# Prologue of a convolution and attention kernel: halves of the taps and of the first image's inputs on other engines, scales inside the first convolution

## The chip, the cores and the metric

One core of one Trainium2 chip. The metric is device time in microseconds of one execution; the median over runs is compared. TensorE multiplies matrices, VectorE (DVE), ScalarE (ACT) and GpSimd (POOL) work element by element, and SyncE (SP) issues DMAs. Each engine takes its instructions in the order in which they are written, and semaphores order the engines among each other.

## The reference

The input `x` is 16 images of 256 channels of 64 x 64 float32. Two layers, each with a residual:

```
x = x + L0(gn(x))    # rotated 3x3 convolution in 8 groups of 32 channels
x = x + L1(gn(x))    # linear attention with cubed features, 8 heads, and a 5x5 depthwise convolution of v
L0: pooled = mean(x); angles = tanh(mlp(pooled)) * pi/4
    w = bilinear rotation of base_kernel by the image's angle
    out = grouped_conv(x, w) * sigmoid(mlp2(pooled))
L1: q, k = relu(x Wq + bq), relu(x Wk + bk), both over softplus(scale_param), cubed, with the norm kept
    out = (q (k^T v) z + depthwise5x5(v)) Wproj + bproj
gn: normalisation over 32 groups of channels
```

## The kernel before

Channels lie on partitions. Factors of matrix products are held as two float16 parts, a high half (rounded) and a low half (what is left), and a product is three matmuls (high x high, high x low, low x high); each operand is scaled by a power that comes from its maximum (`a_w` for the projection's weights, `a_t` for the taps, `a_p`, `a_r`, `a_o`).

The work is written out by hand, engine by engine. A loop over images runs the attention of image b together with the convolution of image b+2. Ahead of it stands the prologue, which is all that the change touches; it handles images 0 and 1 in full and the statistics of image 2. Its parts, in order:

1. Statistics of image 0 (`pixel_stats`, `deviations`, `spreads`, `variance`, `tail`), its pooled means and two small MLPs (`squash` on ScalarE is their tanh, sigmoid and sines), the rotation of its kernel on GpSimd (`rotation(0)`, 27 steps in a chain), and the blocks of rotated weights written to BD by DMA (`weights` on SP's queue, `late_weights` on ScalarE's, 8 issues each; `wt_in` counts them).
2. `softplus` of the head scales, on VectorE with two `exponentials` on ScalarE.
3. The same statistics and MLPs for image 1.
4. `largest_taps`, `largest_weights`, `largest(1)`, `largest_biases`, `scales`: chains of VectorE instructions in which each waits for the one before it. `largest(1)` is two round trips to TensorE.
5. The first convolution (image 0): 8 groups g of two halves q. `high(c, g)` on VectorE zeroes the borders of a plane and casts it to float16, `conv_low` on GpSimd makes its low half, `convolve` is 12 matmuls of 512 columns into bank VA[q], `conv_out` evicts it into the pixels, `result_stats` takes statistics, `shift` on ScalarE adds a bias, `store_x1` stores. Planes have three slots: `high(0, g+3)` waits until both halves of group g are convolved. `rotation(1)` runs on GpSimd meanwhile, with `conv_low(0, 3..7)` between its steps.
6. The second convolution (image 1), the statistics of image 2, and from group 4 on the attention inputs of image 0: units of 512 positions in two slots, each normalised on ScalarE (`attn_input`), cast to its high half on VectorE, its low half on GpSimd, after which SP may load the unit two further on (`next_unit`).
7. `squash(2)` and the first `squares` of the loop.

The taps of the depthwise convolution (`toeplitz`, 12 chunks of 128 x 1024 float32) come through three slots (PL and two parts of SL). ScalarE makes the high half of a chunk (`taps`), VectorE the low half (`low_taps`), and SP loads the chunk three further on when the low half is there (`load_taps`). Scaled weights are split likewise (`split`, `split_bias`): ScalarE the high halves, VectorE the low ones.

Of the kernel before, what the change touches and what calls it, by code (L numbers as in the profile page):

```python
# [5 lines left out]
def conv_then_focused_attention(  # L6
# [58 lines left out]
    with ctx:  # L65
# [129 lines left out]
        t_rdy, tp_act, tp_rdy = sem("t_rdy"), sem("tp_act"), sem("tp_rdy")  # L195
# [59 lines left out]
        TPM = TP[:, :, :, :, :].rearrange("p c k a n -> p (c k) a n")  # L255
        KS = K23[:, :, :, :].rearrange("p k a n -> p k (a n)")
# [64 lines left out]
        def _(sp):  # L321
# [22 lines left out]
            def load_taps(i):  # L344
                if i >= 3:
                    sp.wait_ge(tp_rdy, i - 2)
                    carry(sp)
                sp.dma_start(taps_tile(i), toeplitz[:, i * PIX:(i + 1) * PIX]).then_inc(taps_in[i % 3], 16)
# [60 lines left out]
            def first_convolution():  # L409
                for g in range(3):  # L410
                    planes_after(0, g + 3, g + 1)
                for g in range(GROUPS):
                    if 1 <= g <= 5:
                        for i in (2 * g + 1, 2 * g + 2)[:CHUNKS - 2 * g - 1]:
                            load_taps(i)
# [12 lines left out]
            def second_convolution():  # L428
# [6 lines left out]
                for s in range(4):  # L435
                    sp.wait_ge(x1_out[s], X1_IN * 2)
                    carry(sp)
                for u in range(2):
                    load_unit(0, u)
# [14 lines left out]
                sp.wait_ge(tp_rdy, CHUNKS)  # L454
                carry(sp)
# [75 lines left out]
            for g in range(4):  # L531
                sp.wait_ge(s0_rdy, 2 * g + 2)
                carry(sp)
                load_stats(1, g)
            sp.dma_start(dt32, dw_taps[0, :].partition_broadcast(P)).then_inc(t_in, 16)
            sp.dma_start(DWB[:, :], dw_b[0, :].partition_broadcast(P)).then_inc(t_in, 16)
# [5 lines left out]
            for g in range(4, GROUPS):  # L542
                sp.wait_ge(s0_rdy, 2 * (GROUPS + g - 4) + 2)
                carry(sp)
                load_stats(1, g)
            for i in range(3):
                load_taps(i)
# [4 lines left out]
            for g in (0, 1):  # L552
                load_stats(2, g)
            weights(0)
# [158 lines left out]
        def _(dve):  # L713
# [81 lines left out]
            def largest_taps():  # L795
# [6 lines left out]
                over(a_t, m_t, 16384.0)  # L802
                dve.sem_inc(t_rdy, 1)
# [30 lines left out]

            def low_taps(i):
                dve.wait_ge(tp_act, i + 1)
                hi, lo = (TPM[:, 8 * i:8 * i + 8, a, :] for a in range(2))
                v.scalar_tensor_tensor(lo, taps_tile(i).rearrange("p (m n) -> p m n", m=8), a_t, hi,
                                       ALU.mult, ALU.subtract).then_inc(tp_rdy, 1)
# [118 lines left out]
            def high(c, g):  # L958
# [8 lines left out]
                if g >= slots:  # L967
                    dve.wait_ge(conv_full, 2 * (GROUPS * c + g - slots) + 2)
                dve.wait_ge(cx_rdy, 6 * (GROUPS * c + g + 1))
# [16 lines left out]

            def attn_input(c, u, h):
                dve.wait_ge(xn_rdy, c * 2 * NU + HALVES * u + h + 1)
                hi = XHL[:, 0, h, u * UNIT:(u + 1) * UNIT].rearrange("p (y m x) -> p y m x", y=4, m=4)
                v.tensor_copy(hi, U[:, u % 2, h].rearrange("p m y x -> p y m x")).then_inc(h_rdy, 1)  # L990
# [181 lines left out]
            modulation_back(0)  # L1172
            for g in range(3):
# [9 lines left out]
            largest_taps()  # L1183
            dve.wait_ge(w_in, 16 * N_W)
            largest_weights()
            largest(1)
            largest_biases()
            scales()

            for g in range(GROUPS):  # L1190
                for q in range(2):
# [6 lines left out]
                    if q == 1 and g < 2:  # L1198
                        split(g, wq32[:, g, :], WQ[:, 0, g, :], WQ[:, 1, g, :], a_w)
                    if q == 1 and g == 2:  # L1200
                        split(2, wp32, WP[:, 0], WP[:, 1], a_p)
                    if q == 1 and g == 3:
# [608 lines left out]
```

## Time and profile before

| what | value |
|---|---|
| median of 3 runs | 3855.68 us (3854.17 to 3865.21) |
| profiled execution, its own time | 3868.91 us |
| its span, first to last instruction | 3867.1 us |
| TensorE, busy share of the span | 91% |
| VectorE | 71% |
| ScalarE | 69% |
| GpSimd | 41% |
| mean granted TensorE clock | 0.978 |

The busy times are means over the whole kernel, of which the prologue is the first 265 us; the loop over images has the rest. A row of the timeline is one instruction or several of one form in a row; what stands in brackets is how long the engine was idle before it, and what ended that.

### The profile page before, as it was taken

How to read it: one execution, taken by the hardware profiler on the slowest of the kernel's cores; microseconds unless marked ns; L12 is line 12 of the kernel's file. 1: busy time of each engine (PE TensorE's matmuls, PEld its weight loads, DVE VectorE, ACT ScalarE, POOL GpSimd, SP SyncE). 2: the span in 40 equal slices, each digit the busy share in tenths (PEclk: the TensorE clock that was granted, in tenths of full speed). 3: DMA queues.
4: the chain of work that ended last, by engine and by line, in shares of the span. 5: the costliest groups of instructions: out<-in, count | busy, mean ns of one | idle time of the engine just before them, and what ended most of it. 6: DMA issues, size and time to landing. Idle time of an engine off the chain costs nothing.

```text
span 3867.1 us, 94623 instructions
## 1 busy us (share of the span) xinstructions
PE 3532.3 (91%) x27988; PEld 2857.3 (74%) x27988; DVE 2762.7 (71%) x6715; ACT 2651.2 (69%) x7096; POOL 1596.4 (41%) x1557
## 2 busy tenths in 40 slices
PE   1679999999999999999999999999999999999897
PEld 1248787777877778787777878777787777878786
DVE  7776776767677676777767677676767767575747
ACT  2347676766777677677766767676676767677675
POOL 4551443615345261544526254361535436150402
PEclk9889999999999999999999999999999999999999
DMA  6652634436353453635446263443626344360302
GB/s 217 210 182 73 187 118 139 141 116 177 101 171 111 138 170 91 192 112 151 128 122 190 78 189 112 141 144 114 194 79 184 111 137 135 92 184 13 110 12 77
DMA packets 560058, 516.59 MB, mean 134 GB/s; under 512 B 97601, under 2 KB 491969, under 8 KB 559553
## 3 DMA queue, kind: packets, MB, share of 16 engines
q1 hardware_dynamic: 555200, 508.99, 43.6%
q8 instruction: 230, 3.77, 0.4%
q14 instruction: 276, 2.25, 0.2%
q10 hardware_dynamic: 4352, 1.57, 0.2%
HBM read 351.06 MB, written 134.22 MB: 125 GB/s over the span
## 4 chain that ended last, share of the span: by engine, by line
PE 57%; DVE 12%; issue 11%; ACT 9%; DMA 6%; POOL 2%; SPq 2%; DVEq 1%; ACTq 0%; POOLq 0%
PE F L1541 11%; PE SM L1524 9%; PE VAB L1541 7%; PE F L1580 6%; PE T L1552 5%; PE VAB L1580 5%; DMA PL<-xp 5%; PE PP L1632 4%; PE VAB L1610 3%; ACT K L1308 3%; PE F L1543 2%; PE T L1601 2%; DVE F L996 1%; PE T L1620 1%; SPq L352 1%
## 5 line engine op out<-in xcount | busy, mean ns | idle before, releaser
L1541 PE MATMUL F<-WQ,XHL 128*128 128x256 f16 x6144 | 817.3, 274 | 27.4 <-ACT V L1345 19.1
L636 POOL TENSOR_TENSOR SL<-PL,SL 128x1122 f16<-128x1122 f32 x112 | 259.8, 2320 | 1067.2 <-DVE SL L970 1067.2
L661 POOL TENSOR_TENSOR XR<-XR,V 128x512 f32<-128x512 f32 x256 | 325.9, 1273 | 898.0 <-DVE XR L1057 898.0
L1541 PEld LDWEIGHTS F<-WQ,XHL 128*128 128x128 f16 (+1 forms) x6144 | 601.0, 98 | 103.7 <-issue 33.7
L1314 ACT ACTIVATE K<-K,SCAL 128x256 f32<-128x256 f32 x1024 | 512.6, 505 | 192.2 <-DVE K L1002 191.8
L1308 ACT ACTIVATE K<-F,SCAL 128x256 f32<-128x256 f32 x1024 | 474.8, 469 | 242.9 <-DVE F L996 240.0
L1524 PE MATMUL SM<-SL,BD 128*128 128x512 f16 x2688 | 634.9, 385 | 0.0
L1002 DVE TENSOR_TENSOR K<-K,F 128x512 f32<-128x512 f32 x512 | 350.4, 684 | 273.6 <-ACT K L1308 138.8
L1524 PEld LDWEIGHTS SM<-SL,BD 128*128 128x128 f16 x2688 | 260.9, 97 | 284.2
L996 DVE TENSOR_TENSOR F<-F,FL 128x512 f32<-128x512 f32 x512 | 353.6, 691 | 157.3 <-PE F L1543 152.9
L1632 PE MATMUL PP<-XR,WP 128*128 128x256 f16 x3072 | 385.5, 276 | 48.9 <-DVE XR L1075 48.9
L1541 PE MATMUL VAB<-WQ,XHL 128*128 128x256 f16 x3072 | 420.7, 279 | 6.1 <-DVE V L1022 6.1
L1632 PEld LDWEIGHTS PP<-XR,WP 128*128 128x128 f16 x3072 | 299.6, 99 | 94.6 <-DVE XR L1075 57.9
L1541 PEld LDWEIGHTS VAB<-WQ,XHL 128*128 (+1 forms) x3072 | 308.2, 100 | 48.6 <-DVE V L1022 6.4
L1610 PEld LDWEIGHTS VAB<-KVS,VT 128*128 128x128 f32 x2048 | 263.1, 190 | 102.9 <-issue 42.8
L1610 PE MATMUL VAB<-KVS,VT 128*128 128x132 f32 x2048 | 282.0, 281 | 46.5 <-ACT VT L1356 46.0
L652 POOL TENSOR_TENSOR XHL<-U,XHL 128x512 f16<-128x512 f32 x256 | 296.9, 1161 | 55.9 <-POOL XHL L645 43.2
L1552 PE MATMUL T<-VT,K 128*128 128x129 f32 x2048 | 283.4, 282 | 39.0 <-DVE K L1014 38.7
L979 DVE SCALAR_TENSOR_TENSOR RX<-SM,MODC,RX 128x512 f32<-128x512 f32 x224 | 167.6, 748 | 182.0 <-PE SM L1524 181.9
L1552 PEld LDWEIGHTS T<-VT,K 128*128 128x128 f32 x2048 | 255.6, 196 | 51.0 <-DVE K L1014 48.2
L1543 PE MATMUL F<-BQ,ONES 128*128 128x256 f16 x1024 | 280.4, 274 | 0.0
L1580 PE MATMUL F<-V,TP 128*128 128x248 f16 (+1 forms) x2304 | 277.9, 275 | 0.0
(202 smaller groups left out, 6858.4 us busy)
## 6 DMA issues: line engine op xcount, KB each, us to landing
XR<-xr SPq DMA_DIRECT2D x132, 512.0 KB, 5.3
U<-x SPq DMA_DIRECT2D x256, 256.0 KB, 3.5
XR<-x SPq DMA_DIRECT2D x256, 256.0 KB, 4.2
out<-XR SPq DMA_DIRECT2D x256, 256.0 KB, 3.7
PL<-xp SPq DMA_DIRECT2D x112, 561.0 KB, 3.9
RX<-xr SPq DMA_DIRECT2D x118, 512.0 KB, 3.8
x<-RX SPq DMA_DIRECT2D x448, 128.0 KB, 2.7
BD<-RX SPq DMA_DIRECT2D x240, 96.0 KB, 2.2
```

The lines of the kernel that those rows point to most:

```text
L661: g_.tensor_tensor(o, o, fm, ALU.add).then_inc(o_rdy, 2)
L996: v.tensor_tensor(f, f, fl, ALU.max).then_inc(f_max, 1)
L1002: v.tensor_tensor(K3[:, p, :], K2[:, p, :], F[p][:, :], ALU.mult).then_inc(f_cube, 1)
L1308: a.activation(K2[:, p, ts], F[p][:, ts], ACT.Square, scale=inv_a, accum_out=S2[:, 2 * p + t:2 * p + t + 1]).then_inc(f_sq, 1)
L1314: a.activation(K2[:, p, t * C:(t + 1) * C], K3[:, p, t * C:(t + 1) * C], ACT.Square, scale=inv_a, accum_out=S6[:, 2 * p + t:2 * p + t + 1] ...
L1524: ins = t_.matmul(conv_bank(c, q)[:, :], BD[:, j, HALVES * wa + h, sx, P * sy:P * (sy + 1)], half[:, xa, 16 * q + sy:16 * q + sy + 16, sx: ...
L1541: t_.matmul(o, XHL[:, xa, h, at], WQ[:, wa, h, c0:c0 + C], start=(k == 0), stop=False)
L1543: ins = t_.matmul(o, ONES[:, :], BQ[:, c0:c0 + C], start=False, stop=True)
L1552: ins = t_.matmul(T[h][:, 0:P + 1], K3[:, p, t * C + h * P:t * C + (h + 1) * P], VT[:, p, t, h, 0:P + 1], start=False, stop=False)
L1580: ins = t_.matmul(bank[:, lo:hi], TP[:, c, d, ta, :], V[:, c, va, lo + sh:hi + sh], start=(k == 0), stop=(k == 8))
L1610: ins = t_.matmul(VA[t][:, 0:HALVES * KVC].rearrange("p (g h f) -> p g h f", h=HALVES, f=HPH)[:, :, h], QT[:, p, h, t * P:(t + 1) * P], KV ...
L1632: ins = t_.matmul(PP[:, h * C:(h + 1) * C], WP[:, wa, kk, h * P:(h + 1) * P], OT[:, xa, kk, 2 * P * p:2 * P * (p + 1)].rearrange("p (y m x ...
```

## The change

- **Taps.** The low half of a chunk is made by TensorE and ScalarE: TensorE multiplies the float32 chunk by `AID` (the identity times `a_t`) and adds the high half times `NID` (minus the identity, float16) in banks T[0] and T[1], 512 columns each; ScalarE evicts both to float16. Chunks 0 to 5 stand on ScalarE between `exponentials` and `root(1)` and on TensorE behind `modulation(0)`; 6 to 8 behind `squash(1)` on ScalarE and ahead of the first convolution on TensorE; 9 to 11 behind its groups 0 to 2. `tp_rdy` now counts two for each chunk.
- **Scales.** `largest_taps` goes ahead of `high(0, ..)` on VectorE. `largest_weights`, `largest_biases`, `largest(1)` and `scales` go behind groups 0, 1, 2 and 3 of the first convolution, and the splits behind groups 5, 6 and 7. On TensorE `largest(1)` stands behind `convolve(0, 3, 1)`.
- **First image's inputs.** The high half of a unit of image 0 is made by ScalarE (`attn_high`) and not by VectorE.
- **Order.** On SP the first three taps chunks are loaded ahead of image 1's statistics and the weights' inputs behind them; chunks 3 to 11 are asked for earlier; `weights(0)` stands behind chunks 6 to 8. `late_weights(0)` goes ahead of `squash(1)`. `high(1, 0)` goes into group 7 of the first convolution.

The diff, with context and spaces at the left cut:

```diff
     kb_rdy = sem("kb_rdy")
-    t_rdy, tp_act, tp_rdy = sem("t_rdy"), sem("tp_act"), sem("tp_rdy")
+    t_rdy, tp_act, tp_mm, tp_rdy = sem("t_rdy"), sem("tp_act"), sem("tp_mm"), sem("tp_rdy")
...
+    AID, NID = U2[:, 0, 0:P], U2[:, 0, P:P + P // 2].bitcast(f16)
...
             if i >= 3:
-                sp.wait_ge(tp_rdy, i - 2)
+                sp.wait_ge(tp_rdy, 2 * (i - 2))
...
                 planes_after(0, g + 3, g + 1)
+            for i in range(9, CHUNKS):
+                load_taps(i)
             for g in range(GROUPS):
-                if 1 <= g <= 5:
-                    for i in (2 * g + 1, 2 * g + 2)[:CHUNKS - 2 * g - 1]:
-                        load_taps(i)
...
                 carry(sp)
+            sp.wait_ge(tp_rdy, 2 * CHUNKS)
+            carry(sp)
...
                         next_unit(0, u)
-            sp.wait_ge(tp_rdy, CHUNKS)
-            carry(sp)
...
         sp.dma_start(sc32, head_scale[0, :].partition_broadcast(P)).then_inc(sc_in, 16)
-        for g in range(4):
-            sp.wait_ge(s0_rdy, 2 * g + 2)
+        sp.dma_start(dt32, dw_taps[0, :].partition_broadcast(P)).then_inc(t_in, 16)
+        sp.dma_start(DWB[:, :], dw_b[0, :].partition_broadcast(P)).then_inc(t_in, 16)
+        for i in range(3):
+            load_taps(i)
+        for g in range(GROUPS):
+            sp.wait_ge(s0_rdy, 2 * (g if g < 4 else GROUPS + g - 4) + 2)
...
             load_stats(1, g)
-        sp.dma_start(dt32, dw_taps[0, :].partition_broadcast(P)).then_inc(t_in, 16)
-        sp.dma_start(DWB[:, :], dw_b[0, :].partition_broadcast(P)).then_inc(t_in, 16)
...
         sp.dma_start(BPC[:, :], bproj_patch).then_inc(w_in, 16)
-        for g in range(4, GROUPS):
-            sp.wait_ge(s0_rdy, 2 * (GROUPS + g - 4) + 2)
-            carry(sp)
-            load_stats(1, g)
-        for i in range(3):
+        for i in range(3, 6):
...
             load_stats(2, g)
+        for i in range(6, 9):
+            load_taps(i)
...
             over(a_t, m_t, 16384.0)
+            setup(v.tensor_scalar(AID, ID, a_t, None, ALU.mult))
+            setup(v.tensor_scalar(NID, ID, -1.0, None, ALU.mult))
...
-
-        def low_taps(i):
-            dve.wait_ge(tp_act, i + 1)
-            hi, lo = (TPM[:, 8 * i:8 * i + 8, a, :] for a in range(2))
-            v.scalar_tensor_tensor(lo, taps_tile(i).rearrange("p (m n) -> p m n", m=8), a_t, hi,
-                                   ALU.mult, ALU.subtract).then_inc(tp_rdy, 1)
...
                 dve.wait_ge(conv_full, 2 * (GROUPS * c + g - slots) + 2)
+            elif early(c) and (c, g) == (1, 0):
...
+                dve.wait_ge(conv_full, 2 * (GROUPS - 2) + 2)
...
-
-        def attn_input(c, u, h):
-            dve.wait_ge(xn_rdy, c * 2 * NU + HALVES * u + h + 1)
-            hi = XHL[:, 0, h, u * UNIT:(u + 1) * UNIT].rearrange("p (y m x) -> p y m x", y=4, m=4)
-            v.tensor_copy(hi, U[:, u % 2, h].rearrange("p m y x -> p y m x")).then_inc(h_rdy, 1)
...
         modulation_back(0)
+        largest_taps()
...
         tail(1, 1)
-        largest_taps()
-        dve.wait_ge(w_in, 16 * N_W)
-        largest_weights()
-        largest(1)
-        largest_biases()
-        scales()
...
                     take_norms(1)
-                if q == 1 and g < 2:
-                    split(g, wq32[:, g, :], WQ[:, 0, g, :], WQ[:, 1, g, :], a_w)
+                if q == 1 and g == 0:
+                    dve.wait_ge(w_in, 16 * N_W)
+                    largest_weights()
+                if q == 1 and g == 1:
+                    largest_biases()
                 if q == 1 and g == 2:
+                    largest(1)
+                if q == 1 and g == 3:
+                    scales()
+                if q == 1 and 5 <= g <= 6:
+                    split(g - 5, wq32[:, g - 5, :], WQ[:, 0, g - 5, :], WQ[:, 1, g - 5, :], a_w)
+                if q == 0 and g == 7:
+                    high(1, 0)
+                if q == 1 and g == 7:
                     split(2, wp32, WP[:, 0], WP[:, 1], a_p)
-                if q == 1 and g == 3:
                     split_bias()
-                if 2 <= 2 * g + q < 2 + CHUNKS:
-                    low_taps(2 * g + q - 2)
...
         modulation(1)
-        for g in range(3):
+        for g in range(1, 3):
...
                     pixel_stats(2, 2 * g + q)
-                elif q == 1:
-                    for u in (2 * g - 8, 2 * g - 7):
-                        for h in range(HALVES):
-                            attn_input(0, u, h)
...
+        def low_taps(i):
+            for j in range(2):
+                act.wait_ge(tp_mm, 2 * i + j + 1)
+                a.copy(TPM[:, 8 * i + 4 * j:8 * i + 4 * j + 4, 1, :], T[j][:, :].rearrange("p (m n) -> p m n", m=4)
+                       ).then_inc(tp_rdy, 1)
...
+        def attn_high(u, h):
...
+            act.wait_ge(xn_rdy, HALVES * u + h + 1)
+            hi = XHL[:, 0, h, u * UNIT:(u + 1) * UNIT].rearrange("p (y m x) -> p y m x", y=4, m=4)
+            a.copy(hi, U[:, u % 2, h].rearrange("p m y x -> p y m x")).then_inc(h_rdy, 1)
...
         exponentials()
+        act.wait_ge(t_rdy, 1)
+        taps(0)
+        for i in range(1, 6):
+            taps(i)
+            low_taps(i - 1)
+        low_taps(5)
         root(1)
+        late_weights(0)
         squash(1)
-        late_weights(0)
-        act.wait_ge(t_rdy, 1)
-        for i in range(3):
+        taps(6)
+        for i in range(7, 9):
             taps(i)
-        act.wait_ge(ready, 1)
-        for k, (hi, src, s) in enumerate(((WQ[:, 0, 0, :], wq32[:, 0, :], a_w), (WQ[:, 0, 1, :], wq32[:, 1, :], a_w),
-                                          (WP[:, 0], wp32, a_p), (bh16, bq32, a_w))):
-            a.activation(hi, src, ACT.Copy, scale=s).then_inc(hi_rdy, 1)
+            low_taps(i - 1)
+        low_taps(8)
+        halves = tuple(enumerate(((WQ[:, 0, 0, :], wq32[:, 0, :], a_w), (WQ[:, 0, 1, :], wq32[:, 1, :], a_w),
+                                          (WP[:, 0], wp32, a_p), (bh16, bq32, a_w))))
...
                 shift(0, g - 1)
-            if 2 <= g <= 6:
-                for i in (2 * g - 1, 2 * g)[:CHUNKS - 2 * g + 1]:
-                    taps(i)
+            if g < 3:
+                taps(g + 9)
+                low_taps(g + 9)
+            if g == 4:
+                act.wait_ge(ready, 1)
+                for k, (hi, src, s) in halves:
+                    a.activation(hi, src, ACT.Copy, scale=s).then_inc(hi_rdy, 1)
...
+                act.wait_ge(ready, 2)
...
                         attn_input(0, u, h)
+                    for h in range(HALVES):
+                        attn_high(u, h)
...
+        def low_taps(i):
...
+            pe.wait_ge(tp_act, i + 1)
+            for j in range(2):
+                if i:
+                    pe.wait_ge(tp_rdy, 2 * (i - 1) + j + 1)
+                t_.matmul(T[j][:, :], AID, taps_tile(i)[:, UNIT * j:UNIT * (j + 1)], start=True, stop=False)
+                t_.matmul(T[j][:, :], NID, TPM[:, 8 * i + 4 * j:8 * i + 4 * j + 4, 0, :], start=False, stop=True
+                          ).then_inc(tp_mm, 1)
...
             carry(pe)
-            pe.wait_ge(tp_rdy, CHUNKS)
+            pe.wait_ge(tp_rdy, 2 * CHUNKS)
...
                 modulation(0)
-        largest(1)
+                for i in range(6):
+                    low_taps(i)
+        for i in range(6, 9):
+            low_taps(i)
...
                 convolve(0, g, q)
+            if g < 3:
+                low_taps(g + 9)
+            if g == 3:
+                largest(1)
```

## Rows read from the trace of the kernel before

**Rows 1.** Windows by stage: us per engine with (x) instructions, clock, DMA share, GB/s.

```profile
100.80:170.00 69.20, 46.18 (x168) 17.01 (x168) 60.26 (x87) 30.93 (x28) 47.51 (x35) 0.88 0.57 189
...
222.30:265.60 43.30, 27.93 (x121) 14.58 (x122) 31.53 (x63) 19.49 (x28) 21.32 (x17) 0.76 0.61 180
```

**Rows 2.** Timeline before the first convolution: start, duration, engine, line.

```profile
68.09 0.36 DVE L870 COPY GS<-MV 128x16 f32<-128x16 f32 x1
...
72.94 5.37 SPq L301 DMA_DIRECT2D BD<-RX  x8
...
81.77 0.98 DVE L798 TENSOR_REDUCE SCAL<-XHL 128x1 f32<-128x800 f32 x1
...
84.72 1.80 DVE L784 TENSOR_TENSOR XHL<-XHL 128x256 f32<-128x256 f32 x4 [0.15 <-DVE SCAL L737]
...
86.33 0.19 ACT L1287 ACTIVATE SIN<-ZB 128x2 f32<-128x2 f32 x1
...
87.48 3.19 DVE L789 TENSOR_REDUCE S<-XHL 128x1 f32<-128x1536 f32 x3
...
92.87 0.95 DVE L792 TENSOR_REDUCE SCAL<-XHL 128x1 f32<-128x768 f32 x1
...
100.84 0.75 DVE L979 SCALAR_TENSOR_TENSOR XR<-VAB,MODC,XR 128x512 f32<-128x512 f32 x1 [0.27 <-DVE FL L827]
```

**Rows 3.** Timeline, softplus on VectorE and ScalarE beside the first rotation.

```profile
43.42 1.24 DVE L761 TENSOR_SCALAR XHL<-XHL 128x256 f32<-128x256 f32 x1
...
44.70 1.67 DVE L762 TENSOR_TENSOR XHL<-XHL 128x256 f32<-128x256 f32 x1
...
48.19 0.42 ACT L1265 ACTIVATE XHL<-XHL 128x256 f32<-128x256 f32 x1
...
56.61 1.54 DVE L775 TENSOR_TENSOR XHL<-XHL 128x256 f32<-128x256 f32 x1
```

**Rows 4.** Timeline, lengths on TensorE and of a PSUM read on ScalarE.

```profile
92.57 7.15 PE L1524 MATMUL VAB<-V,BD 128*128 128x512 f16 x24
...
121.75 2.83 PE L1524 MATMUL VAB<-V,BD 128*128 128x512 f16 x12 [1.03 <-DVE XR L979]
...
283.62 1.06 PE L1552 MATMUL T<-VT,K 128*128 128x129 f32 x8
...
284.34 0.68 ACT L1325 ACTIVATE V<-VAB,SCAL 128x512 f32 x1
```

**Rows 5.** VectorE by line in 100.8:170: busy us, mean ns, then idle before.

```profile
L838 DVE SCALAR_TENSOR_TENSOR TP<-SL,SCAL,TP 128x1024 f16<-128x1024 f32 x8 | 13.8, 1726 | 1.4 <-ACT TP L1269 1.4
...
L985 DVE BATCH_NORM_STATS2 ST<-XR 128x6 f32<-128x512 f32 x16 | 11.0, 690 | 0.4
L838 DVE SCALAR_TENSOR_TENSOR TP<-PL,SCAL,TP 128x1024 f16<-128x1024 f32 x4 | 9.0, 2244 | 0.9 <-ACT TP L1269 0.8
L970 DVE CAST V<-V 128x1122 f16<-128x1122 f32 x5 | 6.9, 1370 | 0.5
```

**Rows 6.** Timeline, issue of a taps chunk and the ScalarE instruction behind it.

```profile
115.61 0.36 SPq L348 DMA_DIRECT2D PL<-toeplitz  x1
...
119.22 1.15 ACT L1269 ACTIVATE TP<-PL,SCAL 128x1024 f16<-128x1024 f32 x1 [1.12 <-DMA PL<-toeplitz]
```

**Rows 7.** Timeline, units of image 0 and start of the loop, three engines.

```profile
220.61 2.91 ACT L1299 ACTIVATE U<-U,PR 128x512 f32<-128x512 f32 x4
...
226.70 3.66 DVE L990 CAST XHL<-U 128x512 f16<-128x512 f32 x4
...
230.16 3.63 SPq L352 DMA_DIRECT2D U<-x  x4
...
234.07 1.52 ACT L1299 ACTIVATE U<-U,PR 128x512 f32<-128x512 f32 x2 [6.11 <-DMA U<-x]
...
260.88 1.28 ACT L1281 ACT_TABLE_LOAD   x1 [4.21 <-DVE ZB L934]
...
265.59 0.46 ACT L1308 ACTIVATE K<-F,SCAL 128x256 f32<-128x256 f32 x1
```

## The prediction

> **What bounds the kernel now.** I read the views from coarse to fine. The page gives the span, 3867.1 us. The change touches only what happens before the loop over images, so the question is how long the prologue takes. The chain of work that ended last, followed from the start, runs through VectorE first, then through VectorE and TensorE by turns, through waits for loads of planes, and through loads of the units of image 0 until ScalarE starts the first squares of the loop, at 265.6 us [rows 7]. From there on nothing is changed. Everything that the change can win or lose lies in those 265.6 us; one per cent of the kernel is 38.6 us.
>
> The windows give the two convolutions [rows 1]. In the first one (first eviction at 100.84 us, last statistic at 170.0) VectorE is busy for 60.3 of 69.2 us and TensorE for 46.2: VectorE sets the pace, and `low_taps` is 22.8 us of its work in 12 instructions [rows 5]. From the second half of the second convolution on, no engine is full (31.5 of 43.3 us on VectorE): the pace is a round trip, load a unit, normalise, high half, low half, load the next one.
>
> Before the first convolution the timeline [rows 2] shows VectorE alone from 81.6 to 100.8: tap maxima, scaling of weights, maxima, scales. TensorE had finished both first convolutions (24 matmuls from 92.57 for 7.15 us [rows 4]) and stood at the full banks.
>
> **The change, part A: up to the first eviction.** Removed ahead of it: `largest_weights`, `largest(1)`, `largest_biases` and `scales`, 84.72 to 100.84. That is 16.1 us, if TensorE has the first convolution ready earlier. It has not, because `low_taps(6..8)` now stand ahead of it in TensorE's queue, and they wait for ScalarE, whose `taps(6..8)` stand behind `squash(1)`. So the length of that new chain decides. Step by step:
>
> - VectorE does `largest_taps` before `high(0,..)`. It took 84.72 minus 81.56 (0.2 ahead of the reduction at 81.77) = 3.2 us [rows 2]. New in it are two tensor_scalars of 128 columns (AID, NID). The trace has none; below they cost 0.2 (a one-column instruction and its gap), above 1.24, the 256-column one beside busy GpSimd [rows 3]. GpSimd is busy here, but the width is half: 0.7 each. All that follows moves back by 4.6 us.
> - ScalarE leaves `exponentials` at 48.61 [rows 3] + 4.6 = 53.2 and starts on the taps. A chunk costs it 1.15 for the high half [rows 6] and two evictions of 512 columns at 0.68 [rows 4]: 2.4 us with overlap. TensorE has per chunk two float32 matmuls of 512 columns and two float16 ones. Four float32 matmuls of 129 columns (eight records) take 1.06 us, of which 0.16 overlaps what follows [rows 4]: 0.90, so 512 columns are 0.90/4 x 512/129 = 0.89; a float16 one is 2.83/12 = 0.24. A chunk is 2.3 us at 2.4 GHz, and 4.5 at 1.2 GHz, which is the clock of the first matmuls after a pause: 24 took 7.15 where 12 took 2.83 [rows 4].
> - Chunk 0: 54.4 to 58.9 at the low clock. Chunks 1 and 2 follow to 63.4. The other three need loads, which are asked for only when a slot's low half is evicted, and land 3.6 us later (115.61 to 119.22 [rows 6]). Load 3 is asked at 59.5 and lands at 63.3; load 5 waits for the low half of chunk 2, which stands behind `taps(3)` on ScalarE: asked at 65.7, landed at 69.5, high half to 70.6, and TensorE is done with chunk 5 at 73.5. `group_mean(1)` is queued behind it and its input is there at 68.26 [rows 2] + 0.2 + 4.6 = 73.1. The wait costs 0.4, so the shift is now 5.0. Had the clock stayed low, chunk 5 would end at about 82: 9 us instead of 0.4.
> - ScalarE is out of the low halves at 74.2 and loads its root table (1.28) before the variance comes at 76: hidden. `late_weights(0)` (eight DMA issues, 5.4 us on SP's queue [rows 2]) now lies between `root(1)` and `squash(1)`, from 76.6 to 82, while `squash(1)` waits for VectorE until 86.5: hidden. On SP, `weights(0)` is behind `load_taps(6..8)`, which wait for the low half of chunk 5 at 74.2: about 75.5 instead of 72.9, landed 15 us before it is needed. The weights' inputs go from early in SP's queue to behind the statistics of image 1; VectorE wants them only after 105. The three taps loads that move ahead take a place in a busy queue (first 25 us), but what is read next, image 1's statistics, is wanted only when the whole chain of image 0 is through, and the weights' loads, of about the same size, have left that place: nothing.
> - `squash(1)` ended at 86.5 [rows 2], now 91.5. `taps(6)` to 92.7, three chunks on TensorE, the first at the low clock: 4.5 + 2.3 + 2.2 = 101.7. The first convolution, at the high clock by then, 2.8 + 0.2: first eviction at 104.7. Before: 100.84. **A = +3.9 us.** The bounds: 0 (AID and NID at 0.2, no low clock) and +19.3 (low clock throughout: 8.6 more before `group_mean(1)`, 4.5 more in chunks 7 and 8, 2.3 more in the convolution, so about 15.4 above A).
>
> So the 16 us taken from VectorE ahead of the convolution turn into a wait for TensorE, and the work comes back inside it.
>
> **Part B: the first convolution.** A group of VectorE is two evictions (0.7 each, start to start), two statistics (0.6), and for the first five a plane: borders 0.95, and the cast 1.37 on average, 1.45 with GpSimd busy [rows 5]. That makes 5.0. TensorE needs 5.7 for a group, 8.0 for the first three, which carry a chunk of taps.
>
> Group 0: 5.0, 1.3 of waiting until the second convolution frees the slot, and `largest_weights`. That took 5.9 before (84.72 to 90.67 [rows 2]) with GpSimd idle. Now GpSimd is in `rotation(1)`, as it was in `rotation(0)` when six of `softplus`'s two-input instructions of the same 256 columns took 1.67, 1.54 and, on average, 1.43 each [rows 3], against 0.43 for `largest_weights`'s [rows 2]: 10 us. Group 1: 5.0 + 1.4. Group 2: `largest(1)` is answered by TensorE only after chunk 11 and both convolutions of group 3: VectorE arrives 28.6 us after the first eviction, TensorE is free at 33.1, and the exchange takes 2.2 (90.67 to 92.87 [rows 2]); the group is 12.3 long. Group 3: 5.0 + `scales`, 6.5 alone (94.3 to 100.84), some 3 more with its seven two-input instructions blocked by turns: 14.6. Groups 4 to 6: TensorE's 5.7 each, with the splits of WQ inside. Group 7: 5.2 with `high(1,0)`. Sum 16.5 + 6.4 + 12.3 + 14.6 + 17.1 + 5.2 = 72.1, and 65.0 if neither 10 nor 9.5 is lengthened. GpSimd is busy for 47.5 of the 69.2 us [rows 1], so I take 70. **B = +0.8 us.**
>
> The Trainium skill, page "SBUF — State Buffer", section "SBUF: two separate sides", says that VectorE instructions with two SBUF inputs and GpSimd instructions share a port pair as an exclusive lock, so that one waits until the other has ended. The trace agrees with it here, 1.43 against 0.43 us. It speaks against moving such work under `rotation(1)`: by the rule the sum goes by 72.1, without it by 65.0.
>
> What follows the last eviction is as before: shift, stores, weights. `split(2)` and `split_bias` (5.3 us) now come after it, with one plane fewer: VectorE is ready for the second convolution 3 us later than before, but its first eviction there waits for the blocks of weights and TensorE, which come over 10 us after the last statistic. Nothing.
>
> **Part C: the second convolution.** Until its group 4 nothing moves. Then VectorE no longer does 16 casts (four in 3.66 us from 226.7 [rows 7]), and it and TensorE are free to end 10 us earlier; but ScalarE waits for units, and squares come after it. The chain now: ScalarE starts on unit 0 at 220.6; normal and high halves of both halves of a unit are four instructions at 0.7, the second high half ends at 223.5, GpSimd's second low half at 225.5, and the next load is issued then and not at 230.16 [rows 7]: 4.7 us earlier. It lands 3.9 later, as before (230.16 to 234.07). Each of the two further rounds is about 0.8 longer than the 8.8 seen, for the high halves queue on ScalarE: units 6 and 7 are normalised from 248 to 254. Shift of group 7 (1.1), then `squash(2)`, which no longer waits for VectorE (before: its table load at 260.88 [rows 7]): 255 to 259.9. The squares start at 259.9 and not at 265.6. **C = -5.7 us**; bounds -9 (rounds as short as before, high halves hidden in the waits for loads) and -2 (ScalarE's cast with permuted reading at 1.15 instead of 0.7, in three rounds).
>
> **Sum.** +3.9 + 0.8 - 5.7 = -1.0 us. The profiled execution took 3868.9, 1.8 around its span; the median of the runs is 3855.7, 13 us below it, and the difference is applied to that: 3854.7, say 3855. Within 0.3% (11.6 us) is about what a measurement of this kernel can't tell from no change.
>
> **Rivals.** (1) Slower: TensorE stays at 1.2 GHz in `low_taps`. It works in bits of 2 us between waits for ScalarE and for loads. Then A is +19.3 and the sum 19.3 + 0.8 - 5.7 = +14.4: 3870. It decides once both trios run at the low clock; with the first six chunks alone the sum is -1.0 + 8.6 = +7.6. For it: the engine is all but idle from 40 to 90 us. Against: chunk follows chunk, and the 24 matmuls at 92.57, after the same idleness, average 0.30 us where 0.24 is the high clock's and twice that the low one's [rows 4], so the pace had risen on the way. The Trainium skill, page "TensorE: Matmul & The Clock Gate", section "Part 1: The HAM clock gate", has the same two levels, the low one for an idle engine. I give it 0.14.
> (2) Faster: VectorE's relief is kept. A is 0, B is 65.0 - 69.2 = -4.2, C is -9: -13.2, 3842. For it: 22.8 us leave the busiest engine of that stage. Against: the contention above and `largest(1)`'s wait. 0.17.
> (3) The chain of units is not shortened, since the loads are slowed by stores that now come earlier: C is 0, the sum +4.7, 3860. DMA is busy for 61% of that window [rows 1], so less likely: 0.12.
> (4) My forecast, the parts cancel: 0.57.
>
> **From these to the numbers.** Cases (3) and (4) are within 0.3%, and a tenth of the others falls back into it: same 0.70, faster 0.16, slower 0.14. The range takes in most of (1) and (2): 3842 to 3869.
>
> **What would show it.** First eviction at 104 to 106 us and VectorE idle from 86 until then; chunk 5's second matmul ended before 74; `largest_weights` at 9 to 11 us; an idle VectorE of 5 us before `largest(1)`'s first reduction; 68 to 73 us from first eviction to last statistic; the first squares 90 us after that last statistic instead of 95.6. The prediction is wrong if TensorE's chunks take 4.5 us each, if VectorE's two-input instructions take 0.45 in the convolution, or if the casts on ScalarE lengthen a round of units by over 2 us.

## The result, and the profile after

| | before | after |
|---|---|---|
| median of 5 runs, same chip | 3856.42 us (3854.17 to 3865.21) | 3879.44 us (3873.53 to 3882.43) |
| ratio | | 1.0046, 95% interval [1.0033, 1.006] |
| profiled execution, its own time | 3868.91 | 3873.53 |

The kernel became slower: by 0.46%, or 18 us, in the ratio, and by 23 us between the medians of five runs, where 3855 and no measurable change were forecast. Many of the forecast's steps are nevertheless in the profile, and the prologue did not get longer.

First the prologue. The timeline of the kernel after, rows of VectorE:

```profile
103.25 0.75 DVE L979 SCALAR_TENSOR_TENSOR XR<-VAB,MODC,XR 128x512 f32<-128x512 f32 x1 [17.93 <-PE VAB L1553]
...
108.45 5.10 DVE L785 TENSOR_TENSOR XHL<-XHL 128x256 f32<-128x256 f32 x4
...
115.62 3.19 DVE L790 TENSOR_REDUCE S<-XHL 128x1 f32<-128x1536 f32 x3
...
134.53 0.28 DVE L748 TENSOR_REDUCE VT<-PP 4x1 f32<-4x128 f32 x1 [4.23 <-PE PP L1494]
...
168.71 0.69 DVE L985 BATCH_NORM_STATS2 ST<-XR 128x6 f32<-128x512 f32 x1
```

VectorE stands idle for 17.93 us ahead of the first eviction, at 103.25 us where it was 100.84 [rows 2]: the work taken from it has become a wait for TensorE. `largest_weights` now takes 10.36 us (108.45 to 118.81) and not 5.95, because four of its two-input instructions average 1.25 us beside the busy GpSimd, and two more 0.99, where the four took 0.45 each before (1.80 together [rows 2]); the last statistic ends at 169.40, against 170.0 [rows 1].

TensorE in the first chunks of taps, where the forecast's largest risk lay:

```profile
54.30 2.07 PE L1529 MATMUL T<-PL,U 128*128 128x512 f32 x2 [15.85 <-ACT TP L1262]
...
58.32 1.02 PE L1529 MATMUL T<-SL,U 128*128 128x512 f32 x2
```

One float32 matmul of 512 columns (two records) lasts 2.07 us in chunk 0 and 1.02 to 1.10 us from chunk 1 on: the pace doubles on the way, and chunk 5 is done at 72.5 us. The second trio does the same: 2.07 us in chunk 6, 1.02 from chunk 7 on.

The second convolution and the units of image 0 (ScalarE, GpSimd, SP's queue):

```profile
224.22 2.17 POOL L637 TENSOR_TENSOR V<-V 128x1122 f16<-128x1122 f32 x1 [6.19 <-DVE V L970]
...
228.71 4.14 SPq L354 DMA_DIRECT2D U<-x  x4
...
234.12 1.52 ACT L1298 ACTIVATE U<-U,PR 128x512 f32<-128x512 f32 x2 [6.92 <-DMA U<-x]
...
261.83 0.45 ACT L1313 ACTIVATE K<-F,SCAL 128x256 f32<-128x256 f32 x1
```

The first squares start at 261.83, against 265.59 [rows 7]. So in this pair of executions the loop starts 3.8 us earlier, and the kernel is longer all the same (8.4 us from there to the end in this pair: 3609.9 against 3601.5; the profiled execution before was 12.5 us above its median, the one after 5.9 below): the time is lost in the loop over images, whose source did not change but for the count that one wait looks for (`tp_rdy`).

What is new there is in the waits of TensorE, over 500 to 3300 us (waited for: us in total, times, longest):

```profile
PE T L1581 <- DVE K L1009: 30.3, 22, 1.9
...
PE F L1570 <- issue: 11.2, 10, 1.6
```

and before, over the same window (line 1552 is the later 1581, line 1667 the later 1696):

```profile
PE T L1552 <- DVE K L1014: 29.3, 30, 1.5
PE T L1667 <- issue: 10.6, 12, 2.0
```

"issue" is time in which the engine waits for no other engine and no transfer that the profile shows. Before, line 1541 (the later 1570) had 1.4 us in 2 such waits. Such waits are not all new: those ahead of line 1667 were there before, and are 14.1 us in 10 after. One of the new ones, ahead of line 1570, in the timeline:

```profile
1653.04 1.06 PE L1570 MATMUL F<-WQ,XHL 128*128 128x256 f16 x4
1655.01 0.61 PE L1570 MATMUL F<-WQ,XHL 128*128 128x256 f16 x2 [0.91 <-issue]
...
1655.63 1.49 PE L1570 MATMUL VAB<-WQ,XHL 128*128 128x256 f16 x6
...
1659.57 0.82 PE L1570 MATMUL F<-WQ,XHL 128*128 128x256 f16 x6
```

A group of six matmuls is cut in two by 0.91 us with nothing to wait for, and the groups after it last 1.49 us and not 0.82: the windows show a granted clock of 0.53 from 1654 to 1659 us.

### The profile page after: what moved, and what is told of

Its sections match the earlier page's. It is cut to its first block, busy times and chain, and to the rows that moved or that the text cites. A ratio compares the mean times of both kernels' runs of the same rounds, so it can differ in the third digit from the quotient of the medians.

```text
span 3871.7 us, 94791 instructions
## 1 busy us (share of the span) xinstructions
PE 3555.4 (92%) x28060; PEld 2869.4 (74%) x28060; DVE 2731.8 (71%) x6689; ACT 2674.2 (69%) x7136; POOL 1586.0 (41%) x1557
## 3 DMA queue, kind: packets, MB, share of 16 engines
q8 instruction: 231, 3.78, 0.4%
## 4 chain that ended last, share of the span: by engine, by line
PE 64%; DVE 10%; issue 9%; ACT 8%; DMA 5%; POOL 2%; SPq 2%; DVEq 0%; ACTq 0%; POOLq 0%
PE F L1570 12%; PE SM L1553 10%; PE VAB L1570 8%; PE T L1581 6%; PE F L1609 6%; PE VAB L1609 5%; PE PP L1661 4%; DMA PL<-xp 4%; PE VAB L1639 3%; ACT K L1313 2%; PE F L1572 2%; PE T L1630 2%; PE T L1649 1%; PE VAB L1572 1%; DVE K L997 1%
```

## Experiments

The idle time has no releaser and recurs in nearly every image, at one place of the program. So I compared the compiled programs. TensorE's loop over images begins at its instruction 1052 before and 1207 after (the prologue issues 155 more), ScalarE's at 167 and 207, VectorE's at 616 and 589; GpSimd and SP did not move.
All padding is the same harmless instruction, an increment of a semaphore that nothing waits on. Every ratio below is taken against the kernel before on the same chip; the three series ran on four chips.

**First series: padding the old kernel.**

```diff
+            for _ in range(40):
+                act.sem_inc(carried, 1)
             root(0)
...
+            for _ in range(155):
+                pe.sem_inc(carried, 1)
             pe.wait_ge(c_in, 16 * N_C)
```

`e1_act40` has the first part, `e2_pe155` the second, `e3_both` both.

> The kernel before with 40 increments of a semaphore that nobody waits for, put at the head of ScalarE's program, where it is idle for 24 us; the computation is unchanged. It moves the head of ScalarE's loop over images to the place in the instruction stream that it has in the changed kernel (from instruction 167 to 207). Theory P (placement): the loop over images lost time because the start of its body now lies just ahead of a boundary of the instructions' fetching, on ScalarE and on TensorE. Then ScalarE shows an idle of about 1.5 us between the two reads of VAB into VT at the head of nearly every pass, 12 times, TensorE shows no new one, the prologue is as before, and the time is 5 to 20 us above the kernel before: about 3868. Rival W (the work): the loop lost time since the changed prologue leaves the engines in another phase or slows DMA; then 40 increments change nothing and the time is within 3 us of before.

> The kernel before with 155 increments of a semaphore that nobody waits for at the head of TensorE's program, where it is idle for 18 us; the computation is unchanged. It moves the head of TensorE's loop from instruction 1052 to 1207, as in the changed kernel. Theory P: TensorE shows an idle of about 0.9 us inside the first F<-WQ matmuls of most passes, runs at the low clock for some us behind it, ScalarE shows no new idle, and the time is 3 to 15 us above before: about 3864. Rival W: within 3 us of before.

> The kernel before with both: 40 increments at the head of ScalarE's program and 155 at TensorE's; the computation is unchanged. Both loop heads now stand where they stand in the changed kernel, with the old prologue. Theory P: the loop is as long as the changed kernel's, and the prologue is 3.8 us longer, so the time is the changed kernel's plus up to 4: 3876 to 3886. Rival W: within 3 us of before, 3853 to 3860.

`e1_act40`: 3855.81 us, ratio 0.9997 [0.9988, 1.0006]. The new wait of ScalarE is there (15.6 us in 11, ahead of the line that is 1334 in the changed kernel), but costs nothing that shows, where P had 5 to 20 us: that ScalarE has slack there is argued, not measured. `e2_pe155`: 3873.12, ratio 1.0053 [1.0039, 1.0067], with 10.6 us in 12 issue waits at the line in question. `e3_both`: 3875.6, 1.005 [1.0036, 1.0064]. The old kernel thus becomes as slow as the changed one by instructions that do nothing; `e3_both` is at the lower edge of what P gave it. But e2 mixes two things, and so does e3: in e2 the first matmul comes at 24.64 us where it was at 18.72. 155 increments at TensorE's head outlast the wait that should cover them, so some 6 us (0.15%) are a late start. `e12_before_pe155_idle` mends that: 90 at the head, 65 behind `modulation(0)`.

> The kernel before with 155 idle increments on TensorE as in e2_pe155, but 90 at its head and 65 behind the first modulation, where it is idle: in e2 the 155 at the head delayed the first matmul by 6 us, so e2's +0.5% mixes that with the price of the place. Theory P (TensorE's place alone, instruction 1207 instead of 1052): the stall of 1.6 us x 10 ahead of line 1541 is there and the time is 1.0020 to 1.0035 of before, with the first squares at 261 to 266 us. Theory N (the place costs nothing, e2's surplus was its late start and chance): 0.999 to 1.001.

3869.51 against 3861.63, ratio 1.0016 [1.0004, 1.0028]; first matmul at 17.85 us. TensorE's place alone costs 0.16% in the old kernel, less than the 0.20 to 0.35% expected, though its interval reaches into that range, and the issue waits are there:

```profile
PE F L1541 <- issue: 10.8, 10, 1.6
```

**Second series: other places.** `e6_before_pe256` (90 + 166) moves TensorE's loop by exactly one block, `e7_before_pe205` (90 + 115) to instruction 1257. `e4_after_moved` is the changed kernel with 50 on TensorE (1257) and 20 on ScalarE (227); `e5_after_pe101` has 60 + 41 on TensorE (1308, as e6), `e8_after_pe101_act20` also ScalarE's 20.

> The changed kernel with 20 increments at the head of ScalarE's program and 50 at TensorE's; the computation is unchanged. The loop heads move from 207 to 227 on ScalarE and from 1207 to 1257 on TensorE, which by theory P takes them past the boundary that now follows them closely. Theory P: both new idles are gone, the first squares stay near 261.8 us, and the time is that of before less the 3.8 us of the prologue: 3848 to 3856. Rival W: as the changed kernel, 3874 to 3882.

> The changed kernel with 101 TensorE semaphore increments that do nothing, where TensorE is idle (60 ahead of its first work, 41 behind the first modulation). TensorE's program then reaches the loop over images at instruction 1308, which is the old kernel's 1052 plus 256. Theory P2 (what costs the loop time is where TensorE's loop stands against blocks of 256 instructions): the loop is as long as before, so 3857 less the 3.8 us that the prologue gained in the profiles, about 3853. Theory W (the changed work itself makes the loop longer: other phases of transfers and of the first image): e4_after_moved's 3866 stays, 3862 to 3870. Theory A (the extra ScalarE and VectorE positions carry half of it): 3866 to 3875.

> The kernel before with 256 such increments on TensorE in its idle time (90 ahead of its first work, 166 behind the first modulation): the loop is reached at instruction 1308, same place in a block of 256. P2: no change, 3853 to 3861. If the padding itself costs (as the 6 us at the start of e2_pe155, where 155 at the head delayed the first matmul from 18.7 to 24.6 us) the first image starts late by that and the profile shows it; the loop is unchanged. W: no change either. If the absolute position matters or any shift costs: 3865 or more.

> The kernel before with 205 such increments (90 and 115): loop head at 1257, the place that e4_after_moved had. P2: e4_after_moved was 3866 with 3.8 us gained in its prologue, so its loop cost 12.5 us more than the old one; with the old prologue at that place the time is 3866 to 3872. W: that surplus came from the changed work, so 3853 to 3861 here.

> As e5_after_pe101, and 20 increments at the head of ScalarE's program, which in e4_after_moved ended the stall of 1.7 us x 12 ahead of ScalarE's reciprocal root of a head (line 1334). P2 with ScalarE's stall harmless (as e1_act40 showed for the kernel before): the same as e5, within 0.1%. If that stall costs once TensorE's own is gone: 5 to 12 us below e5.

| run | median us | ratio to before |
|---|---|---|
| e4_after_moved | 3865.68 | 1.0023 [1.0013, 1.0034] |
| e5_after_pe101 | 3865.18 | 1.002 [1.0011, 1.0029] |
| e6_before_pe256 | 3858.38 | 0.9999 [0.9989, 1.0008] |
| e7_before_pe205 | 3859.53 | 0.9999 [0.9988, 1.001] |
| e8_after_pe101_act20 | 3868.45 | 1.0035 [1.0013, 1.0057] |

Padding that is hidden in idle time costs nothing (e6, e7), and three versions of the changed kernel are rid of the issue waits at line 1570 (0.7 us in 1; the line is 1572 in e4 and e8) and of half the loss. P missed twice here: it gave e4 3848 to 3856 us and e7, with TensorE's loop at e4's place, 3866 to 3872, since it put all of e4's surplus on TensorE; W's 3874 to 3882 for e4 was missed too. And e7 warns against reading issue waits as a price:

```profile
PE T L1667 <- issue: 20.3, 11, 2.1
```

That is twice the 10.6 us of before at the same line, at a ratio of 0.9999. Some +0.2 to +0.35% stays in all three, whatever TensorE's and ScalarE's places: so far a point for W. e8 was expected within 0.1% of e5 and is 0.15% above it; its interval is wide, as one of its runs took 3916.37, so this decides nothing.

In the profiles of these three there was one other common sign. VectorE at the end of image 0's first pass, in e5:

```profile
329.99 0.69 DVE L997 TENSOR_TENSOR K<-K,F 128x512 f32<-128x512 f32 x1 [1.33 <-PE T L1581]
```

The same instruction one step earlier, at 325.69, waits 0.97 us behind the same matmuls; this one is 0.36 us late. The releaser's name hides it: it is again idle time that nothing explains. It comes back in every pass: over the loop this wait is 1.33 to 1.37 us in 13 passes of e5 and in 13 of the changed kernel, and in none of before. VectorE's loop stands 27 instructions earlier than before in every version with the changed work, so no run had yet tested its place.

**Third series: VectorE's place.** 27 increments on VectorE, where it waits for the first convolution anyway:

```diff
             tail(1, 1)
+            for _ in range(27):
+                dve.sem_inc(carried, 1)
             for g in range(GROUPS):
```

`e9_after_pe101_dve27` is e5 with them, `e13_after_dve27` has them alone, `e10_after_all_back` adds 216 on ScalarE to e9 (100 at the head, 36 behind `exponentials`, 80 behind `low_taps(8)`).

> The changed kernel with TensorE's padding of e5_after_pe101, and 27 idle increments on VectorE where it waits for the first convolution, so that VectorE's loop too stands where the kernel before has it (instruction 616 instead of 589). In the four versions with the changed work VectorE's subtraction of the old state near the end of each image's pass (line 997) starts 0.36 us later behind TensorE (idle 1.33 instead of 0.97 us), and TensorE's next state waits 1.90 instead of 1.54 us. Theory D (that is VectorE's code arriving late, by its place): the 0.36 us and most of the remaining +0.2% are gone: 0.998 to 1.000 of before. Theory W (the changed work, or ScalarE's place): 1.002 stays, and so does the 1.90 us wait.

> As e9, and 216 idle increments on ScalarE in its idle time (100 at its head, 36 behind the softplus, 80 behind the ninth chunk), so that the loops of TensorE, VectorE and ScalarE all stand at the old places plus a multiple of 256. Theory P in full: the loop is the old one and only the prologue differs, 0.9975 to 1.000 of before, no stall ahead of line 1334 and none ahead of line 1570. Theory W: 1.002. If e9 is 1.002 and this is 1.000, it was ScalarE's place.

> The changed kernel with the 27 idle increments on VectorE alone; TensorE's place stays the changed kernel's. If the two places add up (TensorE's +0.26% from after to e5, VectorE's +0.24% from e5 to e9): 1.0015 to 1.003 of before, TensorE's stall ahead of line 1570 there, the 1.90 us wait for line 1009 back at 1.54. If VectorE's place was worth nothing and e9 was chance: 1.004 to 1.005.

`e9`: 3860.03 against 3859.92, ratio 0.9996 [0.9984, 1.0009]. The whole loss is gone, with all of the change's work still in, and the wait of 1.33 us is in none of its passes. Its VectorE and TensorE at the same place:

```profile
330.38 0.69 DVE L997 TENSOR_TENSOR K<-K,F 128x512 f32<-128x512 f32 x1 [0.97 <-PE T L1583]
...
331.73 1.16 PE L1583 MATMUL T<-VT,K 128*128 128x129 f32 x8 [1.54 <-DVE K L1009]
333.70 1.16 PE L1583 MATMUL T<-VT,K 128*128 128x129 f32 x8 [0.82 <-DVE K L1009]
334.80 0.28 PE L1713 MATMUL T<-NOT,ONES 32*128 32x130 f16 x2
```

and e5's TensorE beside it:

```profile
331.34 3.87 PE L1581 MATMUL T<-VT,K 128*128 128x129 f32 x16 [1.90 <-DVE K L1009]
335.14 0.28 PE L1711 MATMUL T<-NOT,ONES 32*128 32x130 f16 x2
```

From the start of the 16 state matmuls to the next ones it is 3.07 us in e9 and 3.80 in e5. The windows from 330 to 336 us tell why: granted clock 1.00 in e9 and 0.72 in e5. Here TensorE went on at 2.4 GHz after a pause of 1.54 us, and after one of 1.90 us the clock fell to its lower level. So 0.36 us of lateness became 0.36 + 0.73 = 1.1 us at this place.

The length of the pause alone does not decide it. In another pass of e9 the pause was 1.54 us too, and the second eight matmuls took 2.09 us and not 1.16, at a granted clock of 0.78 from 1244 to 1250 us:

```profile
1247.94 2.09 PE L1583 MATMUL T<-VT,K 128*128 128x129 f32 x8 [0.81 <-DVE K L1009]
```

From the start of the 24 state matmuls to the next ones (328.38 to 335.14 in e5) it is 6.5 us or more in all 13 passes of e5, and 5.66 to 6.60 in those of e9, with 8 of 13 above 6.1. The means are 6.87 and 6.10: 13 x 0.77 = 10 us, about the 0.24% (9 us) by which the two runs' ratios differ. In the changed kernel and in e13 they are 6.82 and 5.77.

`e13`: 3868.11 against 3861.63, ratio 1.0024 [1.0013, 1.0036]: TensorE's issue waits are back (9.3 us in 10), its longest wait for VectorE's line 1009 is 1.5 us again and not 1.9, and half the loss is there. The places add up: VectorE's is 1.0046 less 1.0024 = 0.22% beside TensorE's, and 0.24% without it (e5 less e9); TensorE's is 0.26% (after less e5) and 0.28% (e13 less e9). These are differences between ratios that were taken apart, mostly on different chips, and each is good to 0.15 to 0.18% (an estimate from the intervals): all four are clear of zero, but their sizes are rough.

`e10`: 3864.26, ratio 1.0012 [1.0002, 1.0023], more than the 0.9975 to 1.000 expected. ScalarE's place again gives no gain (its wait at line 1334 is gone). The 80 increments ahead of ScalarE's work in the convolution hold ScalarE for 4.86 us (idle to 107.44, by "issue"), and TensorE waits 2.55 us for a high half there. The first squares come at 266.07 us, 2.3 after e9's; single executions scatter by as much, but if it is the padding, it is half of the 0.12%, and the rest is within the interval.

**Undoing one part of the order.** `e11_chunks_later` is e9 with chunks 6 to 8 behind groups 0 to 2 and 9 to 11 behind groups 3 to 5.

```diff
-            for i in range(6, 9):
-                low_taps(i)
...
-                if g < 3:
-                    low_taps(g + 9)
+                if g < 6:
+                    low_taps(g + 6)
```

(ScalarE's calls move in the same way; SP asks for chunks 9 to 11 behind the stores of groups 0 to 2.)

> As e9, and chunks 6 to 8 of the taps are split within the first convolution (one chunk in each of groups 0 to 5) instead of ahead of it. TensorE reaches the convolution 7 to 9 us earlier; the first eviction comes at about 98 instead of 103.25 us, and the last statistic 3 to 5 us earlier if VectorE is what orders that stretch. Where the prologue's end follows, 3 to 5 us below e9 (0.9985 to 0.999 of e9); where the second convolution waits for its planes from memory anyway, as at 180.6 us (6.7 us for a transfer), the same as e9.

3864.01, ratio 1.0009 [0.9996, 1.0021]. The first eviction comes at 101.67 us, 3.1 before e9's 104.75, but no earlier, as TensorE now waits for the convolution's weights:

```profile
96.93 7.26 PE L1550 MATMUL VAB<-V,BD 128*128 128x512 f16 x24 [10.98 <-DMA BD<-RX]
```

The last statistic starts at 174.40, 4.2 after e9's 170.25, and the first squares 4.3 later. VectorE's longest wait inside the convolution is 6.63 us, to 165.16, behind chunk 11, which now stands in group 5: TensorE had waited 2.43 us for its high half there, and the chunk ran at the slower pace (1.73 and 1.91 us for its two float32 matmuls). I had expected a gain of 3 to 5 us or none; the medians are 4 us above e9's, but the ratios differ by 0.13% with intervals of 0.12% each, so all that is shown is that there was no gain.

## Why the prediction was wrong, point by point

**The step that failed** is the sentence "From there on nothing is changed. Everything that the change can win or lose lies in those 265.6 us". 155 more instructions on TensorE and 27 fewer on VectorE ahead of the loop moved its code, and the loop became longer by some 0.5% (18 to 23 us): 0.26% by TensorE's place and 0.24% by VectorE's, shown by e5, e9 and e13 in the changed kernel and, for TensorE, by e12 in the old one. That the place acts through the loading of code is inferred; no view shows the loading. None of the rivals was that mechanism. Rival (1) gave the same sign, but not by what happened: its low clock lasted for one chunk in each trio.

**The sum of the prologue, -1.0 us, came out, but by luck.** In the one pair of profiles it is -3.8, but single executions scatter: the first squares start at 265.59, 262.73, 263.68, 260.77 and 266.16 us with the old work (before, e1, e6, e7, e12: mean 263.8) and at 261.83, 263.66, 263.25, 261.36, 263.79 and 263.16 with the new (after, e4, e5, e8, e9, e13: mean 262.8). That is -1.0 with a standard error of about 1. (e2 and e3, at 269.27 and 275.95, started 6 us late and are left out; e10 and e11 changed the order or held ScalarE back.) And e9 is level with before in time: the forecast "parts cancel" is the state of things once the code stands where it stood. But the terms are not those of the forecast. By the same executions A is +5.3 (first eviction at 104.0 for 98.8), B -3.0 (66.3 for 69.3) and C -3.2 (92.5 for 95.7), where +3.9, +0.8 and -5.7 were forecast: the errors of +1.4, -3.8 and +2.5 cancel.

The terms in detail, from after's profile against before's alone:

- **A** was forecast at +3.9 and is +2.4 (103.25 against 100.84). AID and NID took 0.84 and 0.23 us where I charged 1.4, TensorE's second trio and the convolution went as reckoned (12.0 us from its first matmul at 91.30 to the first eviction), and ScalarE evicted 512 columns to float16 in 0.59 us, not 0.68. The step "chunk 5 at 73.5" was 72.5. The bound of +19.3 did not come near.
- **B** was +0.8 and is 66.1 - 69.2 = -3.1. `largest_weights` was right (10.36 for 10), as was TensorE's exchange (4.23 us of idleness for 5). Too much was put on `scales`, 7.6 us and not 9.5, and on the casts of planes: in the first five groups four took 0.75 to 0.89 us and one 1.60, where I took 1.45. Two slips in the working are small beside that: group 0 adds up to 16.3 and not 16.5, and VectorE's arrival at `largest(1)` to 27.9 and not 28.6.
- **C** was -5.7 and is 92.4 - 95.6 = -3.2 (from the last statistic's end to the first squares). The casts on ScalarE took 0.56 us each, less than the 0.7 charged. But the load of units 2 and 3 left at 228.71 and not 225.5: GpSimd had the sum of a plane in its queue (224.22, 2.17 us) ahead of the low halves, and I had put these right behind ScalarE. The load then took 5.4 us and not 3.9 (why is not shown), so the unit arrived at 234.12, as before. The two rounds after took 8.4 us each, not 8.8 + 0.8; before they had been 8.8 and 8.2, so that the last units came at 250.95 for 251.06. So the chain of units was not shortened, as rival (3) had it; that stores were the reason, as it had it, is not shown. Nearly all of the gain, 3.6 us from there to the first squares (10.88 for 14.53), is that of `squash(2)`, which no longer waits for VectorE.

Of the signs listed, VectorE idle from 86 us (85.3), chunk 5 before 74 and `largest_weights` in 9 to 11 us came true, and nearly so the idle time ahead of the reduction (4.23 us for 5); the first eviction (103.25 for 104 to 106), the convolution's length (66.1 for 68 to 73) and the last stretch (92.4 for 90) missed by 0.75, 1.9 and 2.4 us.

What stays open: whether the stalls are waits for code at all, why they sit where they do inside the loop, and so how to place a loop on purpose. Moving by a whole block (e6) and by 205 (e7) was free, 155 was not; that the pattern repeats with 256 is not shown. VectorE's place was tried in the changed kernel only, since its prologue before has no idle stretch that could hide 229 increments.

## What to carry to other kernels

An edit ahead of a hot loop also moves the loop's code. Where the change is worth less than half a per cent, compare the rows "issue" in the waits of the loop, and idle times with an unchanged releaser that grew by a few tenths; then try the new version with idle instructions, hidden in waits, that bring each engine's loop back to its old place or a multiple of 256 instructions behind it, as in e9, before judging the edit itself. An issue wait is a sign and not a price: e7 had 20.3 us of them at one line and lost nothing. And queue what a freed engine hands over behind what the receiving engine already has, as with GpSimd's plane sum in part C.

## What the runs showed of the hardware that was not expected

- Instructions that do nothing, 155 of them ahead of TensorE's loop, made the kernel 0.16% slower (e12), and 256 or 205 of them did not (0.9999 each).
- ScalarE's stall of up to 1.9 us once an image (15.6 us in 11, e1) cost nothing that can be measured, while VectorE's 0.36 us in 13 passes went with 0.24% (e5 less e9). Behind VectorE TensorE was next in the chain, and it lost its clock more often too.
- An increment of a semaphore is not free: 155 at the head of TensorE's program held its first matmul back to 24.64 us (e2), and 80 held ScalarE for 4.86 us (e10).
